# Decoder blends in front of ScalarE's waits, and two VectorE steps of the second read on GpSimd

## What is computed

```
A_neg = -softplus(A_logit); A_bar = exp(delta*A_neg)
B_bar = (A_bar-1)/(A_neg-eps)*B_proj; B_bar_skip = delta*B_skip
h = h*[A_bar, 1] + out*[B_bar, B_bar_skip]
```

## Time and profile before

| | |
|---|---|
| three timed runs | median 1802.63 us (1797.2 to 1807.58) |
| the profiled execution | 1792.48 us, its span 1790.7 us |
| busy share of the span | TensorE 89%, VectorE 76%, ScalarE 51%, GpSimd 32% |
| mean granted TensorE clock | 0.948 |

### The profile page before, as it was taken

How to read it: one execution, slowest core, us unless ns; L and a number is a source line. 1 busy time by engine, 2 the same in 40 slices (tenths; PEclk the granted TensorE clock), 3 DMA queues, 4 the chain that set the end, 5 groups by cost and what they waited for, 6 DMA issues and landing times. The chain is left out here.

```text
span 1790.7 us, 21054 instructions
## 1 busy us (share of the span) xinstructions
PE 1586.8 (89%) x6880; PEld 1046.3 (58%) x6880; DVE 1356.7 (76%) x2078; ACT 914.7 (51%) x1686; POOL 578.1 (32%) x463
## 2 busy tenths in 40 slices
PE   4899999999999999999999988767899767888999
PEld 3466666666666666666666655465455446445444
DVE  7688788788788788788788867586578578678881
ACT  3345455455455455455554453233458776567630
POOL 2246346446446446446446444210110100000000
PEclk9999999999999999999999999979889855898999
DMA  5001101101102102101101000050634200000121
GB/s 183 24 25 59 36 25 59 36 24 59 36 24 59 36 24 59 36 25 59 36 24 48 24 25 23 18 190 37 129 74 69 91 1 1 1 36 1 47 77 41
DMA packets 30963, 84.20 MB, mean 47 GB/s; under 512 B 6006, under 2 KB 7304, under 8 KB 30600
## 3 DMA queue, kind: packets, MB, share of 16 engines
q1 hardware_dynamic: 30856, 82.87, 15.8%
HBM read 70.27 MB, written 12.58 MB: 46 GB/s over the span
## 5 line engine op out<-in xcount | busy, mean ns | idle before, releaser
L518 DVE SCALAR_TENSOR_TENSOR acc<-pj,sc_o,acc 128x1024 f32<-128x1024 f32 x232 | 293.8, 1278 | 89.4 <-PE pj L649 86.1
L628 POOL TENSOR_TENSOR prob<-prob,inv_total 128x512 f32<-128x512 f32 (+3 forms) x256 | 189.6, 745 | 385.4 <-DVE inv_total L560 385.4
L518 DVE SCALAR_TENSOR_TENSOR q_acc<-pj,sc_q,q_acc 128x1024 f32<-128x1024 f32 x224 | 286.2, 1278 | 34.5 <-PE pj L649 29.3
L649 PE MATMUL pj<-ctx_hi,w_o 128*128 128x512 f32 x528 | 237.1, 449 | 25.5 <-ACT spare L407 12.3
L649 PE MATMUL pj<-zT_hi,w_q 128*128 128x512 f32 x512 | 225.6, 441 | 4.0 <-PEq L81 3.1
L649 PE MATMUL pj<-ctx_lo,w_o 128*128 128x512 f32 x528 | 207.9, 394 | 0.0
L461 ACT ACTIVATE prob<-ps,low_max 128x512 f32<-128x512 f32 (+3 forms) x256 | 134.1, 526 | 144.4 <-DVE low_max L553 144.3
L649 PE MATMUL pj<-zT_lo,w_q 128*128 128x512 f32 x512 | 204.5, 399 | 0.0
L703 PE MATMUL ps<-kT,qT 128*128 128x512 f32 (+3 forms) x512 | 185.7, 445 | 10.5 <-ACT prob L461 10.5
L727 PE MATMUL pv<-probT,v 128*128 128x512 f32 (+3 forms) x512 | 169.5, 433 | 0.0
L649 PEld LDWEIGHTS pj<-ctx_hi,w_o 128*128 128x128 f32 x528 | 99.1, 188 | 110.5 <-DVE acc L518 43.0
(11 more groups left out here) (338 smaller groups left out, 3141.0 us busy)
## 6 DMA issues: line engine op xcount, KB each, us to landing
raw_o<-in_w_o SPq DMA_DIRECT2D x33, 512.0 KB, 3.6
raw_q<-in_w_q SPq DMA_DIRECT2D x32, 512.0 KB, 3.6
x_ring<-qk_kept SPq DMA_DIRECT2D x64, 128.0 KB, 5.1
ln_x<-in_x SPq DMA_DIRECT2D x8, 512.0 KB, 6.9
raw_kv<-in_w_k SPq DMA_DIRECT2D x8, 512.0 KB, 3.6
raw_kv<-in_w_v SPq DMA_DIRECT2D x8, 512.0 KB, 4.6
x<-in_x SPq DMA_DIRECT2D x8, 512.0 KB, 6.6
x_kept<-x SPq DMA_DIRECT2D x8, 512.0 KB, 2.9
```

Source lines behind the costliest of these rows:

```text
L518: dve.scalar_tensor_tensor(out=dst, in0=pj[slot][:], scalar=scale, in1=dst, op0=ALU.mult, op1=ALU.add).then_inc(evac_v, 1)
L628: pool.tensor_tensor(prob[:, k % PROBS, 0:w], prob[:, k % PROBS, 0:w], inv_total[:, n:n + 1].to_broadcast([P, w]), ALU.mult).then_inc(norm ...
L649: ins = pe.matmul(pj[slot][:, b * S:(b + 1) * S], lhs, part[:, b * S:(b + 1) * S], start=n == 0, stop=n == 1)
```

## The change

In `write_read` GpSimd gets the skips of tiles 1 to 7 and the rates of tiles 2 to 7, with the same waits inside (`kept`, `new`) and one on `sp_done` for the soft sums; VectorE keeps rates 0 and 1 and skip 0. In the MLP steps' loop ScalarE's blends of step n come ahead of the decoder copies and the silu of step n, in the second write ahead of the iteration's copies. Quarters, merges and TensorE's order are as before.

```diff
--- before.py
+++ after.py
@@ -2004,6 +2004,12 @@
         def _(pool):
             wr.one_row(pool)
             rd.weights(pool)
+            for i in range(1, NT):
+                pool.wait_ge(wr.sp_done, 1 if i < half else 2)
+                wr.skip(pool, i)
+                if i + 1 < NT:
+                    pool.wait_ge(wr.sp_done, 1 if i + 1 < half else 2)
+                    wr.rate(pool, i + 1)
 
         @block.tensor
         def _(pe):
@@ -2103,11 +2109,11 @@
                 if i == NT:
                     deq.blend(act, Q_MLP)
             for n in range(MLP_IN_READ, len(STEPS)):
+                for q in range(mlp_quarter(n), mlp_quarter(n + 1)):
+                    deq.blend(act, q)
                 if n in MLP_TURNS:
                     deq.copy(act, MLP_TURNS[n], p_w, fT)
                 gated(n)
-                for q in range(mlp_quarter(n), mlp_quarter(n + 1)):
-                    deq.blend(act, q)
 
         @block.vector
         def _(dve):
@@ -2142,10 +2148,6 @@
                     wr.total(dve, i)
                     if i + 2 == half:
                         wr.soft_sum(dve, link, 1)
-                    if i + 2 < NT:
-                        wr.rate(dve, i + 2)
-                    if i + 1 < NT:
-                        wr.skip(dve, i + 1)
                 if i >= 1:
                     rd.finish(dve, link, i - 1)
                 if i > MLP_FROM:
@@ -2274,6 +2276,8 @@
                 deq.copy_half(act, u, p_w, fT)
 
             for i in range(half + 3):
+                for q in range(w2_quarter(i), w2_quarter(i + 1)):
+                    deq.blend(act, q)
                 if 1 <= i <= half:
                     wr.copy_od(act, i - 1)
                 if 2 <= i <= half + 1:
@@ -2282,8 +2286,6 @@
                     wr.copy_delta(act, i - 3)
                 if i - 1 in W2_TURNS[0]:
                     half_tile(W2_TURNS[0][i - 1])
-                for q in range(w2_quarter(i), w2_quarter(i + 1)):
-                    deq.blend(act, q)
             wr.soft(act, 0)
             wr.copy_od(act, 4)
             half_tile(12)
```

## The result

The changed kernel takes 1812.48 us (median of 14 runs, 1805.47 to 1821.34), the kernel before 1800.9 us (14 runs, 1796.13 to 1807.58). The ratio is 1.0071, 95% interval 1.0055 to 1.0087: slower by 0.7%. The forecast was 1818.0 (1804 to 1828).

The account below looks back on a forecast made before the run. Loops between engines, no saturated engine, bound the touched stages. 15.4 + 1.6 - 1.6 = +15.4 us on the profiled 1792.5 gave 1807.9; with timed runs' median 10 above, 1818.0 us, range 1804 to 1828.

Parts of the forecast that it names:

- Part B: MLP steps, blends ahead of copies and silu: a loop silu, product, merges, blends closes, +15.4 us.
- The walk of the twelve steps: MLP steps 4 to 15 timed one by one by assumed durations, ending at 1613.4 against 1598.0.
- Two signs: MLP steps: silus 6 to 15 would come 4 to 6 us apart, VectorE idle before products 9 to 15.
- the clock behind the second stop: MLP steps, decoder turn 4: lower TensorE clock after standing 8.7 us would cost 2.7 us.
- R1: MLP steps: rival that blends just fill the waits, their merges being done; 1799.4 us, chance 0.11.
- R4: MLP steps: rival that the loop closes at half the cost, +8 us, 1810.6 in all; chance 0.18.
- Part A: Read's tiles, rates and skips on GpSimd: blocking with VectorE costs +1.6 us, bounds -1.3 and +7.
- R2: Read's tiles: rival that VectorE's busy time decides, 8.4 us of work moved; 1791 us, chance 0.04.
- R3: Read's tiles: rival of slow GpSimd, a rate exceeding 2.2 us; forecast plus 5.4, 1823.4 us, chance 0.12.
- Part C: Second write, blends ahead of copies: no loop closes, -1.6 us, bounds -4.6 and 0.
- in front of the first unit: Second write, TensorE's wait before the last matmul's first unit: some 0.3 us shorter.
- the last gap: Tail after the second write: TensorE's last gap would give at most 1.3 us.

Follow-up runs that it names:

- a_only: Only the rates and skips moved to GpSimd, against the kernel before: 1797.86 us, ratio 1.0002.
- a_rate_after_total: a_only with GpSimd waiting for total(i) before it makes rate(i+1): one run, 1802.31 us.
- c_only: Only the second write's blends moved ahead of the copies, against the kernel before: 1799.29 us, ratio 1.0000.
- mended_b_and_c: merges_copies_first plus the change's blend order in the second write: 1791.21 us, ratio 0.9952 to the kernel before.
- merges_copies_first: Kernel before, with MLP merges ahead of products on VectorE and ScalarE's order copies, blends, silu: 1788.3 us, ratio 0.9950.
- merges_copies_again: The same kernel as merges_copies_first, run a second time: 1790.87 us, ratio 0.9952 to the kernel before.

## Why the prediction came out as it did

**Part B, right in its mechanism, 1.1 us too much.** The walk of the twelve steps against the trace. The MLP's stage starts 7.06 us later in after (1549.79 and 1542.73), and this is taken off the measured times:

| starts at | forecast | measured |
|---|---|---|
| silu 6, 7, 8 | 1554.3, 1558.9, 1561.7 | 1554.25, 1558.83, 1561.52 |
| copy of turn 3 | 1566.3 | 1566.15 |
| silu 9 | 1573.6 | 1573.72 |
| silu 10, 11, 12, 13 | 1579.5, 1584.0, 1588.6, 1591.3 | 1579.66, 1584.08, 1588.68, 1591.37 |
| copy of turn 4 | 1596.0 | 1595.98 |
| silu 14, 15 | 1603.3, 1609.3 | 1602.30, 1608.22 |
| last keep ends | 1613.4 | 1612.35 |

Up to turn 4 every step is within 0.2 us; TensorE's stops were forecast as 6.5 and 8.7 and are 6.28 and 8.76. Two signs were worded more widely than the walk: silus 8 and 13 come 2.69 us behind the ones before them and not 4 to 6, and VectorE waits in front of products 9, 10, 12, 14 and 15, not 11 and 13. The term that was mis-sized is the clock behind the second stop: I took 2.7 us. From the turn at 1603.67 to the next step at 1609.16 are 5.49 us, against 3.93 undisturbed (0.49 and 3.44), so 1.6. The same difference carries through silus 14 and 15 to the end. The price of B is 14.34 us for 15.4. R1 (blends just fill waits) and R4 (half the cost) fall: silus 10, 11 and 12 are 4.42 and 4.60 us apart, not 3.44.

**Part A, the mechanism right, the size too large: 0.45 for 1.6.** The blocking on `total(0)` is there, 1.18 us instead of 1.6. I had taken 1.9 us for an undisturbed rate; it is 1.65 (1485.85), less than 1.5 times the 1.27 of the earlier trace rows, so runs of three elements cost nothing that shows; a skip is 0.73 for 0.6. Beside tile 3, `total` is 0.46 longer and L1681 0.56, forecast 0.9 and 0.6: less than the 1.32 of rate and skip taken away, so 0.3 is won there. This gives 0.88, and the turn of tile 3's `h` is 0.86 later. Some 0.4 was won back behind that tile, at one place: the distance stays 0.85 up to the first MLP group (1518.94 and 1511.48) and is 0.47 at the next turn, with a granted clock of 0.75 for 0.70 between. The forecast had no term for this. It is in both kernels with A in this form (4.99 and 5.22 us against 5.42 to 5.65 without A), so it seems to belong to A, though two traces are few and the mechanism isn't shown. a_only's stage was 0.21 longer than before's.

A surprise in size: rates that meet VectorE take 2.42 to 2.44 us, five of the six, so GpSimd waits too. VectorE gave up 8.4 us of work, but its busy time fell by 3.9 only (69.95 to 66.02): the other 4.5 came back as instructions made longer.

R2 (VectorE's busy time decides) falls: with 4 us less on the busiest engine the stage didn't get shorter, and in a_rate_after_total, with VectorE busy 71.16 us, 1.2 more than before, it was 0.4 shorter. By the Trainium skill (Perfetto Trace Analysis, Identifying the Most-Contended Engine) the busiest engine was the one to relieve; this stage disagrees, since a loop over three engines sets its period. R3 (a rate over 2.2 us) met its condition, as the rates took 2.4, but not its price: a rate is that long only beside VectorE's instructions, and it is over before the next `total` except at tiles 0 and 3, whose longer `total` is counted above. The condition had been put on the wrong number.

**Part C, right in its largest certain term, and the nearness of 1.1 to 1.6 is in part luck.** The wait at `copy_low(3)` fell by 0.54 (forecast 0.55). The stage is 1.34 shorter and the tail 0.24 longer. Of the 1.34, 0.51 is the time of `main(0)` (7.38 for 7.89, granted clock 0.71 for 0.67), which isn't C. Forecast 0.3 in front of the first unit: 2.16 became 1.88, but in c_only and mended_b_and_c, which have C too, it is 2.12, so this term isn't shown to be C either. What repeats is the 0.54: c_only's stage is 0.56 shorter, and its whole time doesn't move. Forecast up to 1.3 by the last gap: it stayed, 1.36 for 1.34, so that term was wrong. A unit's copy ends that gap, and the earlier chain doesn't feed it.

**The sum.** 0.45 + 14.34 - 1.10 = 13.7 for 15.4. The forecast of 1818.0 is 5.5 above 1812.48: 1.7 from this sum, 1.7 because three runs had put before at 1802.63 and fourteen put it at 1800.9, and the last 2.1 is the difference between the two traces' 13.7 and the medians' 11.6 (12.8 by the ratio). No run shows a cause for it; scatter of the clock is a guess. That A came 1.2 lower and C 0.5 less helpful than forecast cancels in part, which is luck.

**What I didn't see ahead.** The forecast named the loop's members and priced them, but not that one of them, product in front of merges, was a free choice. Turned round, together with the copies' place, it makes the same idea gain 8.6 to 9.0 us by the ratios of merges_copies_first, merges_copies_again and mended_b_and_c (0.9950, 0.9952, 0.9952), and 6.7 with A added (0.9963). No run has the merges in front of the products and ScalarE's order as in before, so what that turn does by itself isn't shown.

## What to carry to other kernels

Before work is put in front of an engine's wait, follow what that work itself waits for: if it leads over another engine back to the thing that the first wait was for, a loop closes, and its period replaces the cheap wait. Then look at each order inside that loop that is a free choice (here product or merges first) and at which queued copy another engine needs soonest (here the PSUM bank of a turn), and turn these with it. An engine's chain that got 4.5 us earlier is worth only what the engine that sets the end had waited for it.

## What the runs showed of the hardware

- **GpSimd and VectorE block each other both ways.** A rate of 1.65 us (tile 3 of after) took 2.42 to 2.44 beside VectorE's instructions with two SBUF inputs, a `total` of 1.23 took 2.41, and L1709 of 0.95 took 2.35 beside a rate. I had expected it of VectorE only. A 128 x 2 form also stretched: L822, also with two inputs, is 0.16 us undisturbed and 1.44 beside a rate (1478.18 in a_rate_after_total).
- **The clock that TensorE gets back after a stop isn't a function of the stop.** After 2.14 us in turn 3, turn and `m_g` took 1.11 and 3.13 in before (granted clock 0.58), 0.66 and 1.88 in a_only (1.00). After 3.26 us, the 16 matmuls of `main(0)` took 5.29, 6.99, 8.13, 8.14 and 8.33 in five executions (granted clock 1.00, 0.76, 0.65, 0.65, 0.63), of which 5.29 and 8.13 are of the same kernel; after 6.12 us they took 6.74 to 8.07. These runs don't show what decides it. Against 5.22 us undisturbed, one such stop was worth 0.1 to 3.1 us of clock, so a difference under some 3 us between two traces can't be put down to a change until this is taken out.
